# Own PSUM banks for batch 0's probability transposes, and another order of ScalarE's and VectorE's work around them

## The reference

```python
# step 0: pooling with a mask (prefix, postfix, or all but itself, by a type id)
scores = tanh(x @ W1 + b1) @ v
p = softmax(where(mask, scores[:, None, :], -1e30), axis=-1)      # 2048 x 2048 a batch
x = x + einsum('bjl,bld->bjd', p, x) / count
# step 1: a three-point stencil along rows and along channels, plus zR * x * (1 - x)
# step 2: adapter 512 -> 128 -> 512 with relu, chosen by an id, then a layer norm
# step 3: gates, two causal moving averages, products with 512 x 512 weights, a layer norm
```

## Time and profile before

| | us |
| --- | --- |
| time, median of 3 runs (lowest, highest) | 695.63 (695.38, 696.37) |
| the profiled execution's own time | 696.12 |
| its span | 694.3 |
| TensorE busy | 655.5 (94%) |
| VectorE busy | 551.6 (79%) |
| ScalarE busy | 369.9 (53%) |
| GpSimd busy | 175.5 (25%) |

### The profile page before, as it was taken

The page is one execution under the profiler, slowest core; times in us unless marked ns, Lnnn a source line. Parts: engine busy times, 40 slices in busy tenths (PEclk is TensorE's granted clock), DMA queues, the critical chain, the costliest instruction groups (busy, mean ns, idle before and its releaser), DMA issues.

```text
span 694.3 us, 8219 instructions
## 1 busy us (share of the span) xinstructions
PE 655.5 (94%) x2848; PEld 493.6 (71%) x2848; DVE 551.6 (79%) x792; ACT 369.9 (53%) x759; POOL 175.5 (25%) x268
## 2 busy tenths in 40 slices
PE   3969989899799999999999999999999999999996
PEld 1535445468577878787878787888787878787875
DVE  3576776959998898889879988898799749974955
ACT  1143348684567457645764476447635753574245
POOL 5003410311066005510550055015401210121001
PEclk9999999999999999999999999999999999999999
DMA  7996999997117852563257325733473230032001
GB/s 208 323 345 217 257 259 273 341 316 216 20 33 130 170 92 73 120 112 61 78 134 123 61 74 118 112 62 84 113 106 61 39 84 0 1 51 72 1 0 60
DMA packets 51575, 86.83 MB, mean 125 GB/s; under 512 B 8256, under 2 KB 10304, under 8 KB 51406
## 3 DMA queue, kind: packets, MB, share of 16 engines
q0 software_dynamic: 16896, 33.56, 30.1%
q1 hardware_dynamic: 31134, 52.74, 20.9%
q10 hardware_dynamic: 3504, 0.01, 0.3%
HBM read 63.22 MB, written 22.04 MB: 123 GB/s over the span
## 4 chain that ended last, share of the span: by engine, by line
PE 61%; DVE 22%; ACT 7%; issue 6%; DMA 1%; SPq 1%; POOLq 0%; ACTq 0%; POOL 0%; DVEq 0%
PE bank L1169 16%; PE bank L1170 16%; PE bank L1171 16%; DVE tr L1738 5%; PE bank L1070 3%; PE bank L1165 3%; DVE tr L1729 2%; ACT mod L854 2%; DVE wgb L1725 2%; DVE wgb L1717 2%; PE bank L1245 2%; DMA xts<-in_xT 1%; DVE tr L1746 1%; ACT wgb L867 1%; PE bank L1276 1%
## 5 line engine op out<-in xcount | busy, mean ns | idle before, releaser
L1738 DVE TENSOR_TENSOR_SCAN tr<-alpha,carry,tr 128x512 f32<-128x512 f32 x48 | 58.8, 1267 | 0.0
L641 POOL TENSOR_TENSOR rs_a<-ss_a,consts 128x1 f32<-128x1 f32 x32 | 15.9, 498 | 147.0 <-ACT junk_f L821 146.6
L1169 PE MATMUL bank<-th,wg_l 128*128 128x512 f32 x128 | 52.0, 406 | 0.0
L1169 PE MATMUL bank<-xh,wg_l 128*128 128x512 f32 x128 | 51.9, 406 | 0.0
L1170 PE MATMUL bank<-tl,wg_h 128*128 128x512 f32 x128 | 50.5, 395 | 0.0
L1170 PE MATMUL bank<-xl,wg_h 128*128 128x512 f32 x128 | 50.5, 395 | 0.0
L1171 PE MATMUL bank<-xh,wg_h 128*128 128x512 f32 x128 | 50.2, 392 | 0.0
L1171 PE MATMUL bank<-th,wg_h 128*128 128x512 f32 x128 | 50.2, 392 | 0.0
L873 ACT ACTIVATE carry<-tr 128x2 f32<-128x2 f32 x32 | 6.6, 205 | 80.3 <-DVE tr L1738 80.3
L1725 DVE SCALAR_TENSOR_TENSOR wgb<-wgb,soma 128x512 f32<-128x512 f32 x32 | 22.0, 687 | 30.5 <-ACT wgb L867 30.5
L854 ACT ACTIVATE mod<-bank,bias_n 64x512 f32<-64x512 f32 x32 | 21.9, 683 | 38.3 <-PE bank L1276 37.6
(11 more groups left out here) (290 smaller groups left out, 2016.3 us busy)
## 6 DMA issues: line engine op xcount, KB each, us to landing
x2b<-beside_scratch POOLq DMA_DIRECT2D x12, 1024.0 KB, 9.1
xr<-rows_scratch POOLq DMA_DIRECT2D x10, 1024.0 KB, 10.4
xb<-in_x SPq DMA_DIRECT2D x8, 1024.0 KB, 14.3
result<-xr SPq DMA_DIRECT2D x7, 1024.0 KB, 4.4
beside_scratch<-xts SPq DMA_DIRECT2D x6, 1024.0 KB, 9.8
x2b<-rows_scratch POOLq DMA_DIRECT2D x6, 1024.0 KB, 11.0
x_scratch<-xb SPq DMA_DIRECT2D x5, 1024.0 KB, 10.9
x2b<-x_scratch SPq DMA_DIRECT2D x5, 1024.0 KB, 5.6
```

The costliest lines, as they stand in the source:

```text
L1169: pe.matmul(acc, wl, xh_, start=start, stop=False)
L1738: ve.tensor_tensor_scan(t[:, d], alpha[:, 1 + d:2 + d].broadcast_to([P, GN]), t[:, d], 0.0 if first else carry[:, k, 1 + d:2 + d], ALU.mul ...
```

## The change

Batch 0's probability transposes get a table of banks of their own, `TURNED_PROB`: groups 0 and 1 go to banks 0 and 5, groups 2 and 3 stay in 1 and 2. Their waits follow: group 0 waits for the last tanh of batch 0 that reads bank 0 or 1, group 1 for the g_raw copy that reads bank 5, and groups 2 and 3 for the block-weight evictions of their banks as before. The first two groups of batch 1's hidden layer, in banks 0 and 5, wait for the evictions of these transposes. Pooled product 1, in bank 4, waits for block-weight eviction 1. TensorE now does two groups of probability transposes, two pooled products, the other two groups, and two more products. ScalarE copies the raw block sums ahead of the block exponentials, and takes its evictions in the order block weights 0, replicated sums, probabilities 0, block weights 1 and 2, probabilities 1, block weights 3, probabilities 2 and 3. VectorE does `sums_low` ahead of `normalise` instead of after `params_blend`. No instruction is added or taken away.

```diff
@@ tables @@
             TURNED = ((3, 4, 1, 2), (1, 2, 1, 2))
+            TURNED_PROB = ((0, 5, 1, 2), (1, 2, 1, 2))
@@ ScalarE @@
                     def probT_evict(b, j):
                         act.wait_ge(probT_mm, NG * b + j + 1)
-                        act.activation(probT[:, part(j)].rearrange("p c l -> p (c l)"), bank[TURNED[b][j]][:],
+                        act.activation(probT[:, part(j)].rearrange("p c l -> p (c l)"), bank[TURNED_PROB[b][j]][:],
                                        ACT.Copy).then_inc(probT_cp, 1)
...
                     act.wait_ge(pool_const, 7)
+                    sums_raw(0)
                     block_exps(0)
-                    sums_raw(0)
                     prob_exps(0)
+                    bw_evict(0, 0)
                     sums_hi(0)
-                    for j in range(NG):
-                        bw_evict(0, j)
-                        probT_evict(0, j)
+                    probT_evict(0, 0)
+                    bw_evict(0, 1)
+                    bw_evict(0, 2)
+                    probT_evict(0, 1)
+                    bw_evict(0, 3)
+                    probT_evict(0, 2)
+                    probT_evict(0, 3)
                     mix_local(0)
@@ TensorE @@
                         if b == 0 and j >= 2:
                             pe.wait_ge(hid_act, j - 1)
-                        elif b == 1 and j == 0:
-                            pe.wait_ge(hid_act, NG)
-                        elif b == 1 and j == 1:
-                            pe.wait_ge(g_cp, 1)
+                        elif b == 1 and j < 2:
+                            pe.wait_ge(probT_cp, j + 1)
                         elif b == 1:
                             pe.wait_ge(hid_act, n - 1)
...
                     def prob_transposes(b, j):
                         pe.wait_ge(prob_act, NG * b + j + 1)
-                        if b == 0:
+                        if b == 0 and j == 0:
+                            pe.wait_ge(hid_act, NG)
+                        elif b == 0 and j == 1:
+                            pe.wait_ge(g_cp, 1)
+                        elif b == 0:
                             pe.wait_ge(bw_cp, j + 1)
...
-                            last = pe.transpose(bank[TURNED[b][j]][:, P * i:P * i + P], prob[:, GT * j + i],
+                            last = pe.transpose(bank[TURNED_PROB[b][j]][:, P * i:P * i + P], prob[:, GT * j + i],
                                                 ident[:])
...
                         elif n == 1:
-                            pe.wait_ge(probT_cp, 2)
+                            pe.wait_ge(bw_cp, 2)
...
-                    for j in range(NG):
-                        prob_transposes(0, j)
-                    for c in range(4):
-                        pooled(0, c)
+                    prob_transposes(0, 0)
+                    prob_transposes(0, 1)
+                    pooled(0, 0)
+                    pooled(0, 1)
+                    prob_transposes(0, 2)
+                    prob_transposes(0, 3)
+                    pooled(0, 2)
+                    pooled(0, 3)
                     hidden(1, 0)
@@ VectorE @@
                     normalise_out(0)
+                    sums_low(0)
                     normalise(0)
                     params_blend()
-                    sums_low(0)
                     params_cols()
```

## The result

The changed kernel takes 691.32 us (median of 5 runs, 690.95 to 692.79) against 695.56 (5 runs, 695.01 to 696.37) before: ratio 0.9935, 95% interval 0.9917 to 0.9952. The forecast of 692.0 (690.1 to 694.4) holds it. The profiled execution took 691.58 us, its span 689.8.

The account below looks back on a forecast made before the run. Bound: an early chain of four TensorE-ScalarE turns over shared banks, then gapless TensorE work. Turns 2.5 plus halved clock about 1.4 gave 3.9 us; from 696.12 and 695.63 that left 692.2 and 691.7, taken as 692.0 (690.1 to 694.4).

Parts of the forecast that it names:

- Step 1: ScalarE copies raw block sums first, at 37.65 us instead of 38.84; block exponentials 0.22 late, no cost but no cover left.
- Step 2: Two groups of probability transposes get own banks; ScalarE becomes the slower side, replicated sums evicted 41.88 to 42.46 us.
- Step 3: VectorE's low half goes first, starting at 42.5 us; its preparing work ends at 48.6 instead of 47.63, setting the first tile.
- Step 4: TensorE's pooled product 0 starts at 43.2 us instead of 49.12; product 3 waits for VectorE, 49.5 instead of 53.38.
- The clock: Halved TensorE clock behind the turns, at the last transposes and first pooled product: about 1.4 us of the gain.
- the turns: TensorE and ScalarE alternating over shared banks in four turns: 2.5 us of the gain, after the loss on VectorE.
- No fall in the new gap: TensorE's clock stays whole despite a 2.0 us gap just before product 3; a fall would cost 1.7 us.
- Rival A: The second clock fall, at the product at 92.46 us, goes too: 1.4 us more gain, 690.6 us; chance 0.13.
- Rival C: Part of the gain is lost where transfers meet, near the x2 transposes: 693.4 to 693.6 us, 695.0 with both; chance 0.12.
- My margin of 2.3 us: Before the x2 transposes at 108.61 us, an accumulating DMA lands at 106.3, 2.3 us ahead.
- Rival D: More banks buy nothing: the path crosses to ScalarE and VectorE, first tile as late as before; 695.9 us; chance 0.06.
- Rival E: Slower: main loop's first group comes at other moments and the clock falls there, up to 1.7 us a fall; chance 0.04.

Follow-up runs that it names:

- raw sums late: Changed kernel with ScalarE copying the raw block sums behind the block exponentials again; 690.97 us, ratio 0.9931.
- the run with the sums first: Changed kernel with ScalarE evicting the replicated sums before block weights 0; 690.80 us, ratio 0.9924.
- The fill: Kernel before with one unused product of constants in each of TensorE's first three waits of the turns; 693.71 us, ratio 0.9967.
- the control: The kernel before, run again without any edit; 695.51 us, ratio 0.9996.
- The run with the low half late: Changed kernel with VectorE's low half back behind norm and blend parameters; 694.14 us; with three unused products in TensorE's idle time, 692.74 us.
- the kernel with the rows later: Changed kernel with VectorE's blend parameters, columns and rows put behind the fourth pooled tile; 689.59 us, ratio 0.9911.
- the two orders without banks: Kernel before with raw sums copied first and low half ahead of the norm, but shared banks and old evictions; 696.43 us, ratio 1.0010.
- both edits together: Changed kernel with replicated sums evicted first and parameters, columns and rows behind the fourth pooled tile; 689.38 us, ratio 0.9914.

## Why the prediction was right, point by point

All my absolute times are 0.8 us early from the start, by the first load. Taken off, the steps read as follows.

- **Step 1.** g_raw at 38.45 forecast, 38.53 measured. Right, and right that it is worth nothing (raw sums late).
- **Step 2.** Replicated sums at 42.68 forecast, 42.76 measured. Right. That ScalarE would be the slower side held too; the run with the sums first moved the interval by the 0.48 that the step names.
- **Step 3.** Low half at 43.3 after a wait of 0.8, rows done at 49.4; measured 43.37, 0.88 and 49.35. Right. What the step did not see is what it implies: once VectorE sets the first tile, everything in its queue that the tile does not need should go behind it. That is worth another 1.7 us.
- **Step 4.** Product 0 at 44.0 forecast, 44.31 measured; I left out the weight load there. It did not matter, since product 3 waits for VectorE: 50.3 forecast, 50.19 measured. The interval gained 3.99 against a sum of 3.9. The gap ahead of product 3 was 1.48 and not 2.0, mostly by the later product 0.
- **The clock.** The term was mis-sized. I priced the first fall at 1.4 us from one trace. The fill prices it at 2.1 us in the medians, and the control's profile shows why: 20.33 against 18.02, 2.3 us, where the fall is longer. The other term, the turns, is 18.02 - 15.42 = 2.6 against my 2.5. By these the sum would have been 4.9 or less, and 4.2 to 4.5 was measured; what remains between them is within the spread of single runs. So the number came out close in part because the one trace at hand had the milder fall.
- **No fall in the new gap.** Right: with TensorE idle for 1.48 us before product 3, the clock was 1.00 from 44 to 60 us, and the profiles with the sums first and with the raw sums late, with 1.44 us there, have no fall there either. The run with the low half late shows the other side, at an idle of 3.68 us. The rule of the Trainium skill that I weighed (TensorE: Matmul & The Clock Gate, section What's actually happening), that the clock follows recent work, is borne out by the fills, which change only what TensorE does in the gaps. No run separates the two things that they change at once, the share of time at work and its kind: in the turns all work between the waits is transposes, and each fill is a product.
- **Rival A** came true between the two profiled executions: 92.46 to 108.61 is 16.15 us before, 89.38 to 104.05 is 14.67 after, 1.48 less, and I had put 1.4 and a chance of 0.13. It is no general gain, and it was luck that these two differ in it. Of the five executions three had no fall left and two had at least one, at 690.95 and 692.79 us against 691.01 to 691.58: the times don't sort by it. Nor do those of the kernel with filled turns, where six without a fall have a median of 693.8 and six with one 693.4. What decides the price is where the fall lies. In the kernel before, run again, it lies ahead of the idle time of 2.42 us:

```profile
81.77 1.05 PE L1090 MATMUL bank<-v_sb,hid 128*128 128x1 f32 x8 [1.25 <-DVE wlog L1511]
82.75 3.54 PE L1101 MATMUL bank<-xb,wsel 128*32 128x512 f32 x16
...
93.07 1.10 PE L1165 MATMUL bank<-xb,probT 128*128 128x512 f32 x2 [0.76 <-DVE xb L1565]
```

Its block sums take 3.54 us, where the changed kernel's take 1.92, but the idle time shrinks to 0.76 and takes the loss up. From the last scores (81.77) to the product behind the idle time it is 11.3 us, as in the changed kernel without a fall (78.07 to 89.38), and from product 3 to the x2 transposes 53.76 (53.98 to 107.74) against 53.86. The same holds for the two orders without banks, the low half late (with and without fills), the raw sums late and both edits together, which have their fall there and need 53.75 to 53.86 us for that stretch; the rows later need 54.77, with the wait of 0.82 for the DMA in it. Behind the idle time nothing takes the fall up: 55.23 before (53.38 to 108.61), and 56.90 with the sums first, whose fall there was twice as long.
- **Rival C** did not happen at this size of shift: in the changed kernel the DMA before the x2 transposes is issued at 94.30 and lands 9.1 us later, 0.65 ahead of them at 104.05. It did happen 1.7 us further on, in the kernel with the rows later. My margin of 2.3 us shrank in part because the second fall of the clock was gone, which the transfers do not share in. The chain that ended last in the changed kernel passes through another of the stencil's transfers, but the rest of the program did not become longer by it (rival E):

```profile
122.36 10.23 DMA beside_scratch<-xts
...
132.66 0.70 ACT soma L831
```

- **Rival D**, with the page's "gave no further gain" (the Trainium skill, TensorE: Matmul & The Clock Gate, section HAM oscillation), is refuted here by the two orders without the banks (1.0010) against the whole (0.9935).
- **Rival E** did not appear: the chain from the first x2 transposes to the end is as long as before, 4.56 and 4.5 us gained at its ends. In all profiles of the study the rest of the span takes 585.7 to 586.0 us.

Open is what exactly decides a fall of the clock in batch 1's stretch, and its place: the same idle of 2.42 us had one in one profile and none in another, with the same work around it, and the pause of 1.25 us likewise.

## What to carry to other kernels

Where two engines take turns over a shared PSUM bank, price two things: the turns themselves, and the half clock that TensorE's idling in them may bring to the work behind; a throw-away product in the gap measures the second by itself, and in this kernel it was half of the gain. Look where a fall lies before pricing it: ahead of an idle time long enough to take it up it cost nothing here. After the turns are gone, look at which queue now sets the first result and put behind it all that the result does not need. A margin of a transfer is to be counted against the whole shift, the regained clock included.

## What the runs showed of the hardware that I had not expected

VectorE's scaling of the blend weights, two instructions on 128 x 4 elements that take 0.24 us together in the changed kernel, took 3.45 us where the rows come later:

```profile
49.58 3.59 POOL L587 TENSOR_TENSOR xts<-xb 128x2040 f32<-128x2040 f32 x1 [38.67 <-DVE xb L1577]
...
49.82 3.45 DVE L1626 SCALAR_TENSOR_TENSOR blend_w<-blend_w,blend_t 128x4 f32<-128x4 f32 x2
```

This is the kernel with both edits. GpSimd's channel sum started 0.24 us earlier and ended at 53.17, and VectorE went on at 53.19. The kernel with the rows alone later has the same two rows, 0.66 us later. The Trainium skill (SBUF — State Buffer, term "shared port pair") says that VectorE and GpSimd share a pair of ports by an exclusive lock and that the loser blocks fully; this row agrees, with 3.2 us over the 0.24. Here TensorE has no wait between 49 and 74 us, so I see no cost in this trace, but a small step is not free to go anywhere.

The other surprise is the size of the clock's effect in a stretch of TensorE work as thin as four groups of transposes: 2.1 us of 695 for three gaps of 1.25 us.
